# Turning 32x32 tiles of x on VectorE instead of transposing x on TensorE

## What is computed

```python
msg = jnp.concatenate([x[src], edge_attr], axis=1) @ W1 + b1      # (50000, 96) @ (96, 128)
agg = jax.ops.segment_sum(msg, dst, num_segments=100000)
out = jnp.concatenate([x, agg], axis=1) @ W2 + b2                 # (100000, 192) @ (192, 64)
x = _layernorm(x + out, axis=-1)
```

## Time and profile before

| | us |
|---|---|
| median of three runs | 1029.17 |
| lowest, highest | 1028.0, 1034.58 |
| the profiled execution | 1031.75 |
| its span in the profile | 1030.0 |

### The profile page before, as it was taken

How to read it: one execution, slowest core, us unless ns; L and a number is a source line. 1 busy time by engine, 2 the same in 40 slices (tenths; PEclk the granted TensorE clock), 3 DMA queues, 4 the chain that set the end, 5 groups by cost and what they waited for, 6 DMA issues and landing times.

```text
span 1030.0 us, 25989 instructions
## 1 busy us (share of the span) xinstructions
PE 667.1 (65%) x8086; PEld 601.0 (58%) x8087; DVE 411.6 (40%) x945; ACT 446.2 (43%) x2113; POOL 398.7 (39%) x422
## 2 busy tenths in 40 slices
PE   3194557657656775676575677657656756579764
PEld 3174556547646664565475567546646646579753
DVE  7273334334325333333343234533433433337443
ACT  1013434535536454354364346534534534366422
POOL 8664443443443335334434433443443443620000
PEclk8576876876768677677687668867877876678666
DMA  2121322322333223223223223332232332233101
GB/s 62 27 53 40 84 61 66 87 71 66 77 80 98 59 74 88 59 69 91 63 76 87 61 66 85 95 74 68 73 82 61 88 76 57 65 80 90 45 22 42
DMA packets 171918, 71.39 MB, mean 69 GB/s; under 512 B 64737, under 2 KB 165615, under 8 KB 171888
## 3 DMA queue, kind: packets, MB, share of 16 engines
q1 hardware_dynamic: 107728, 51.75, 17.3%
q0 software_dynamic: 12544, 12.87, 6.9%
q10 hardware_dynamic: 51616, 6.41, 4.0%
HBM read 45.37 MB, written 25.60 MB: 69 GB/s over the span
## 4 chain that ended last, share of the span: by engine, by line
PE 61%; issue 31%; DVE 2%; another core or an unknown queue 2%; POOL 2%; DVEq 1%; DMA 0%; ACT 0%; ACTq 0%; POOLq 0%
PE ps_y L549 27%; PE ps_y L540 13%; PE ps_z L468 8%; PE ps_x L529 6%; PE ps_t L460 4%; PE ps_y L586 1%; POOL feat L435 1%; PE ps_x L607 1%; PE ps_y L567 1%; DVE onehot_x L962 1%; DMA feat<-in_x,src_idx 0%; DVEq L962 0%; PE ps_y L607 0%; DVEq L240 0%
## 5 line engine op out<-in xcount | busy, mean ns | idle before, releaser
L435 POOL DMA_INDIRECT feat<-in_x,src_idx x392 | 390.1, 995 | 529.3 <-PE ps_t L460 406.3
L549 PE MATMUL ps_y<-z_window,onehot 128*128 128x64 bf16 x5292 | 292.4, 211 | 285.9 <-issue 282.1
L549 PEld LDWEIGHTS ps_y<-z_window,onehot 128*128 128x128 bf16 x5292 | 240.8, 110 | 337.8 <-issue 328.0
L669 ACT ACTIVATE square<-ps_y 128x64 bf16<-128x64 f32 x784 | 162.6, 240 | 401.8 <-PE ps_y L540 399.8
L932 DVE TENSOR_TENSOR onehot<-node_of_col,dst_in_group 128x2304 bf16<-128x2304 bf16 x98 | 133.2, 1359 | 331.1 <-PE ps_y L540 307.2
L540 PE MATMUL ps_y<-wx,x_t 128*128 128x128 f32 x784 | 155.9, 360 | 6.5 <-issue 6.4
L669 ACT ACTIVATION_READ_ACCUMULATOR square<-ps_y 128x1 f32 x784 | 159.6, 225 | 0.0
L540 PEld LDWEIGHTS ps_y<-wx,x_t 128*128 128x128 f32 x784 | 134.8, 259 | 8.2 <-issue 7.6
L468 PE MATMUL ps_z<-wz,feat_t 97*128 97x64 f32 x784 | 100.6, 285 | 4.5 <-issue 4.5
L468 PEld LDWEIGHTS ps_z<-wz,feat_t 97*128 97x128 f32 x784 | 98.7, 204 | 5.6 <-issue 5.2
L812 DVE TENSOR_TENSOR z<-z_rest,z 128x512 f32 (+1 forms) x49 | 33.9, 691 | 134.1 <-ACT z L657 71.8
(11 more groups left out here) (148 smaller groups left out, 244.2 us busy)
## 6 DMA issues: line engine op xcount, KB each, us to landing
xin<-in_x SPq DMA_DIRECT2D x97, 192.0 KB
out<-yout SPq DMA_DIRECT2D x97, 192.0 KB
xin<-in_x SPq DMA_DIRECT2D x99, 64.0 KB
out<-yout SPq DMA_DIRECT2D x99, 64.0 KB
feat<-in_x,src_idx POOLq DMA_INDIRECT x392
feat<-in_edge_attr ACTq DMA_DIRECT2D x97, 64.0 KB
z<-in_src SPq DMA_DIRECT2D x1, 192.0 KB
z<-in_dst SPq DMA_DIRECT2D x1, 192.0 KB
```

Of the source, the lines that this page charges most:

```text
L435: nc.gpsimd.indirect_dma_start(out=feat[h][:, feat_at(k) + c, 0:C], out_offset=None, in_=x[:, :], in_offset=bass.IndirectOffsetOnAxis(ap=s ...
L549: nc.tensor.matmul(ps_y[h][:, col:col + C], onehot[h][:, slot, a, :], z_window[h][:, slot, part * C:(part + 1) * C], start=False, stop=Fal ...
L669: sq = nc.scalar.activation(square[:, q, :], ps_y[h][:, q * C:(q + 1) * C], ACT.Square, accum_out=sumsq[:, h, q:q + 1])
```

## The change

x is loaded so that its 32x32 tiles only have to be turned around in their places. A row of a tile of x (two nodes, 128 values) is cut into four quarters of 32 values; quarter i of 32 rows goes to partitions 32i to 32i+31, at columns 32m to 32m+31 for rows 32m to 32m+31. VectorE's transpose of 32x32 tiles then gives the 128x128 transpose in one instruction for the whole block (128x512). TensorE's transposes of x, the banks' copies on ScalarE and the semaphore `x_used` are gone; the bank `ps_x` is used in the setup only. A block's load is eight DMAs instead of two (four quarters, low part and high part), each piece 128 bytes long in DRAM instead of 512; the first block has 12 more for its cut part, in place of one. `turn_x` stands in VectorE's unit ahead of each block's one-hots, and waits for the load and for `y_done[h]` of the unit before, since it writes `x_t[h]`. The loads wait for `x_ready[h]`.

```diff
+        def low_squares(b, i):
+            at = (BLOCKS - 1 - b) * GN
+            rows = x[at:at + GN, :].rearrange("(p a) c -> p (a c)", a=A)
+            return rows[:, i * SQ:(i + 1) * SQ].rearrange("(m r) c -> r m c", r=SQ)
+
+        def high_squares(b, i):
+            at = LOW + (BLOCKS - 1 - b) * HIGH * GN
+            groups = HIGH if b > 0 else 1
+            rows = x[at:at + groups * GN, :].rearrange("(p a) c -> p (a c)", a=A)
+            return rows[:, i * SQ:(i + 1) * SQ].rearrange("(m r) c -> r m c", r=SQ)
...
             def load_x(k, h):
                 b = 2 * k + h
-                wait_rounds(sp, x_used[h], k)
-                sp.dma_start(xin[h][:, 0, :], low_part(x, b)).then_inc(x_loaded[h], 16)
+                wait_rounds(sp, x_ready[h], k)
+                for i in range(A * C // SQ):
+                    quarter = xin[h][i * SQ:(i + 1) * SQ, :, :]
+                    sp.dma_start(quarter[:, 0, :].rearrange("r (m c) -> r m c", c=SQ), low_squares(b, i)).then_inc(x_loaded[h], 16)
+                    groups = quarter[:, 1:(G if b > 0 else 2), :].rearrange("r g (m c) -> r (g m) c", c=SQ)
+                    sp.dma_start(groups, high_squares(b, i)).then_inc(x_loaded[h], 16)
...
-            def turn_x(k, h):
-
-                pe.wait_ge(x_loaded[h], 16 * transfers(k + 1, h))
-                wait_rounds(pe, x_ready[h], k)
-                for g in range(G):
-                    tr = nc.tensor.transpose(ps_x[h][:, g * P:(g + 1) * P], xin[h][:, g, :], ident[:, :])
-                tr.then_inc(x_used[h], 1)
...
                 dense(G - 1).then_inc(y_done[h], 1)
-                turn_x(k + 1, h)
...
-            def keep_x(u, h):
-                act.wait_ge(x_used[h], u + 1)
-                nc.scalar.activation(x_t[h][:, :], ps_x[h][:, :], ACT.Copy).then_inc(x_ready[h], 1)
...
                 keep_y(u, 0)
-                keep_x(u + 1, 0)
                 keep_y(u, 1)
                 root(u)
-                keep_x(u + 1, 1)
...
+            def turn_x(k, h):
+
+                dve.wait_ge(x_loaded[h], 16 * x_transfers(k + 1, h))
+
+                dve.wait_ge(y_done[h], k + 1)
+                nc.vector.transpose(x_t[h][:, :], xin[h][:, :, :].rearrange("p g c -> p (g c)")).then_inc(x_ready[h], 1)
...
             def unit(u):
-                one_hots(u, 0)
-                one_hots(u, 1)
+                for h in range(2):
+                    turn_x(u, h)
+                    one_hots(u, h)
                 normalize(u)
```

More of the change, by code:

```diff
@@ L58 @@
 EPS = 1e-5
+SQ = 32
 assert BATCHES == BLOCKS == 2 * PAIRS and 0 <= TWICE < P and BLOCKS <= P and G == 4
@@ L210, in gnn_residual_layernorm @@
         x_loaded = sem2("x_loaded")
-        x_used = sem2("x_transposed")
-        x_ready = sem2("x_t_ready")
+        x_ready = sem2("x_turned")
         hots_used = sem2("onehots_used")
@@ L267, in high_part, with cut_squares, x_transfers @@
             return t[at:at + groups * GN, :].rearrange("(g p a) c -> p g (a c)", g=groups, p=P, a=A)
+        def low_squares(b, i):
[7 more added lines that the diff above has]
+            return rows[:, i * SQ:(i + 1) * SQ].rearrange("(m r) c -> r m c", r=SQ)
+        def cut_squares(i, m, parts):
+            rows = x[CUT:N, :].rearrange("(p a) c -> p (a c)", a=A)
+            return rows[m * SQ:m * SQ + parts, i * SQ:(i + 1) * SQ]
         def cut_part(t):
             return t[CUT:N, :].rearrange("(p a) c -> p (a c)", a=A)
+        def x_transfers(k, h):
+            return 2 * A * C // SQ * k + (A * C // SQ * -(-CUT_PARTS // SQ) if h == 0 and k > 0 else 0) \
+                if isinstance(k, int) else 2 * A * C // SQ * k + A * C // SQ * -(-CUT_PARTS // SQ) * (1 - h)
         def transfers(k, h):
@@ L318, in load_x @@
                 b = 2 * k + h
-                wait_rounds(sp, x_used[h], k)
-                sp.dma_start(xin[h][:, 0, :], low_part(x, b)).then_inc(x_loaded[h], 16)
-                if b == 0:
[L322 to L325, removed]
+                wait_rounds(sp, x_ready[h], k)
[4 more added lines that the diff above has]
+                    sp.dma_start(groups, high_squares(b, i)).then_inc(x_loaded[h], 16)
+                if b == 0:
+                    for i in range(A * C // SQ):
+                        for m in range(-(-CUT_PARTS // SQ)):
+                            parts = min(SQ, CUT_PARTS - m * SQ)
+                            sp.dma_start(xin[h][i * SQ:i * SQ + parts, 2, m * SQ:(m + 1) * SQ],
+                                         cut_squares(i, m, parts)).then_inc(x_loaded[h], 16)
             for h in range(2):
@@ L360, in _ @@
                         load_x(k, h)
-                    else:
-                        sp.wait_ge(x_used[h], PAIRS)
-                        sp.sem_inc(x_loaded[h], 32)
                 if k >= 2:
@@ L611, in _ @@
             pe.wait_ge(s_wready, 3)
-            for h in range(2):
-                turn_x(0, h)
             for h in range(2):
@@ L719, in _ @@
             edge_round(LAG + 1)
-            for h in range(2):
-                keep_x(0, h)
             act.wait_ge(s_opened, 2)
```

## The result

The changed kernel takes 995.88 us (median of four runs, 993.5 to 996.11), beside 1030.87 us (1028.0 to 1034.58) for the kernel before: a ratio of 0.965, 95% interval 0.962 to 0.968. 993 us was forecast.

What follows compares the result with a forecast made beforehand. Each 20.2 us round was taken as GpSimd's gathers with their trail, then TensorE's own work. TensorE 39, last units +2, collisions -2, SyncE -2, start -1 gave 36 us off 1031.75: 996, or 993 as run median; range 975 to 1012.

Steps and rivals of the forecast that it cites:

- TensorE's gain, 0.87 us a unit, 39 us: TensorE's chain without transposes of x: 0.43 us (slow clock) plus 0.44 us a unit, over about 45 units.
- The rival of the full 1.29 us: TensorE's clock rises with work done, not time: 1.29 us gained a unit, 974 us in all; chance 0.17.
- some 6 us after the crawl ended: When TensorE's clock rises, counted from when small matmuls beside the gathers stop coming singly; expected unchanged without the transposes.
- The sign set for the idle time behind a series: Expected in a round's chain: next first gather 0.9 us sooner after the last one's end, 9.1 us for 10.0.
- The last four units, 2 us gained: At the end, four units wait at places for VectorE: 2 us more gained for them, between 0 and 5.
- ScalarE, nothing: ScalarE's 98 removed copies of 0.58 us are not on the chain, so no gain was counted.
- VectorE's transpose, 0.65 us, under cover: VectorE's transpose ahead of the one-hots takes 0.65 us; TensorE needs the windows later, so nothing waits directly.
- The collisions, 0.30 us lost and 0.25 gained a round: Gathers beside later window copies lose 0.30 us, beside later `normalize` gain 0.25: net 0.05 a round, 2 us lost.
- the rival: The gathers eat the gain: copies hit each round's second gather, `normalize` gains nothing, 29 us lost, 1022 us; chance 0.15.
- 2 were allowed for the rounds with two units: SyncE's 8.6 us a unit against some 6.5 without gathers: 2 us lost in two-unit rounds, between 0 and 13.
- The rival of SyncE as the bound: Issues up to 1.37 us make SyncE's unit 24 us against 20.2: 1200 us; chance 0.13 together with another slower rival.
- covered by over 10 us: SyncE's loads for a block, 3.3 us plus a landing, are wanted only a round later, so hidden.

Runs made afterwards that it cites:

- the dead transposes: The changed kernel with four unread TensorE transposes per block put back behind dense: 1.006 of the kernel before at 1044.4 us, 1.122 where that takes 645 us.
- two_loads_2: The changed kernel with x loaded by the old two DMAs a block, node sums wrong: 999.4 us, 0.957 of the kernel before at 1044.4 us.
- two_loads: The changed kernel with x loaded by the old two DMAs a block, node sums wrong: 650.3 us, 1.007 of the kernel before at 645.0 us.

## Why the prediction was right, and where it was not

**What bounds the kernel.** Right for the first condition: a round is the gathers' part plus TensorE's own. I read the crawl as a property of the kernel. It comes with a condition outside it: the same program ran without it. The one row that could have warned is the earlier trace rows itself, where a matmul without a dependence waits 0.29 and 0.49 us on "issue".

**TensorE's gain, 0.87 us a unit, 39 us.** Right: 0.90 us a round between dense and `turn` in the two traces, 0.92 us a unit (41.5 us) by the dead transposes. The argument behind it holds as well: the transposes took 1.30 us of a round, and other matmuls, moved down into the slow stretch, gave 0.43 of it back (forecast: 1.29 and 0.42). The rival of the full 1.29 us is out. What I had from one round only is the place of the rise, "some 6 us after the crawl ended": over the rounds the mean is 5.0 us before and 4.5 after, and it comes no later with less work in front of it. The sign set for the idle time behind a series, 0.9 us less, came out at 1.4 (9.27 and 7.87).

**The last four units, 2 us gained.** Wrong in sign: 5.7 us lost from the 49th series on. I costed them for TensorE and left SyncE out, though its loads stand ahead of `free_yout` there as anywhere; two_loads_2 gives most of it back.

**ScalarE, nothing.** Nothing of it shows: with the copies out and the transposes back, the kernel is not faster than before. No run takes the copies out alone; as the loads cost 9 us of a net 5.7, a few us for ScalarE aren't excluded.

**VectorE's transpose, 0.65 us, under cover.** 0.71 us; TensorE waits for windows 7.3 us in all in the changed kernel, 3.7 before. Covered. In the second condition it and the rest of the change, without the loads, cost 0.7% (two_loads).

**The collisions, 0.30 us lost and 0.25 gained a round.** In the traces: gathers that overlap window copies went from 12 with 5.5 us of stretch to 45 with 21.3, 0.35 us a round lost; those that overlap `normalize` from 75 with 13.3 us to 74 with 8.3, 0.11 gained. Net 0.24 us where 0.05 was written. My reason for 0.30, copies at the gather's start more than at its end, has it the right way round: the later in a gather the copies start, the longer it gets (last section). One of the two long gathers that I set beside the page's rule, the one of 1.40 us, ran beside a product and not a copy.

Whether a longer gather lengthens the round one for one, as the sum and the rival had it, stays open. Over all rounds the series grew by 0.31 us and dense started 0.27 us sooner, which speaks against it; in the rounds in which dense starts behind the last gather the series grew by 0.24 us and dense starts 0.13 us later (0.26 by the medians), which doesn't. The pace of the crawl moves both, and no run holds it still. What is out is the rival's price: with 29 us lost the kernel would have come out at 1022 us. The Trainium skill's page SBUF — State Buffer, section Who interferes with whom, is borne out in that the gather is held up by the copies (1.21 us beside the copies at 591.16). It is not borne out in the order: the page gives the shared ports to whoever issues first, for its whole instruction, and here the gather had begun first and was still the one to wait. In the second condition, where from the 7th series on GpSimd waits for nothing, a longer gather goes into the round in full.

**SyncE.** Issues 0.47 and 0.43 us (medians of L346 and L348), a block 3.9 us instead of 3.3, since I took the low part's issue from the first of a pair. Packets 267,312 for 265,000; the queue's share rose by 8.2 points, as forecast. Cost: 9 us where 2 were allowed for the rounds with two units and 1 for the start.

**The sum.** 39 + 2 - 2 - 2 - 1 = 36; measured 41.5 - 5.7. TensorE's term was right for its reason. The rest was luck in part: the net of the others, 3 us forecast and 5.7 measured, came near although the end was wrong in sign and the loads and collisions were too small.

**The rival of SyncE as the bound** was given a point of decision: 1.1 us an issue against a round of 20.2 us. It came true in the second condition with issues 0.49 us apart, since the round fell to 10.9. That is the step of the prediction that doesn't carry: "covered by over 10 us" took the round of 20.2 us as given. The number that I should have set beside it is how short a round the other engines can make: eight gathers, 10 us, were in the rows.

## What to carry to other kernels

A cost is hidden only as long as the thing that hides it stays slow. Work out each hidden queue (here SyncE: 16 issues and 4 stores, 9.8 us a unit) against the fastest round that the other engines can make, not against the round seen. A stretch of "issue" on the bounding engine is no property of the kernel until runs at other times show it too; before a change is kept that pays on one queue for time on that engine, both kernels want timing where that stretch is gone. And an experiment that takes away a wait can hand the chain to the next queue: compare the time, not the wait.

## What the runs showed of the hardware

- One program, 1030 and 645 us. In the slower condition small matmuls come singly, 0.72 or 1.43 us apart, from some 3 us behind the start of the first gather of a series until 1.3 us behind the end of the last (means of the kernel before); in the other 54 of them take 1.75 us beside gathers. What sets the condition isn't known; it held for whole groups of runs, and the chip with the number 15 showed both.
- A gather of 0.94 us takes longer by a fixed pattern when the four window copies of a block start during it, at least 0.05 us behind its start: in all 848 such cases of the fourteen traces it ended 0.08 us (0.077 to 0.089) ahead of the last copy. So it took 0.95 us with copies that start at once and up to 2.13 us with copies that start at its end; 1.60 us in the earlier trace rows (copies 0.70 us behind its start), 1.70 us at 403.03 (0.80 us behind).
- A gather that starts while one of the products of `normalize` (128x512 float32, two inputs) has been under way for over 0.05 us, and goes on for 0.13 us more, ends 0.82 us behind that product: all 317 cases without window copies in the fourteen traces lie within 0.01 us of it, up to 1.44 us for the gather. A product that begins behind the gather's start costs it nothing. Between 0 and 0.05 us ahead both occur; in two_loads_2, where most begin 0.03 to 0.04 us ahead, the gathers take 0.94 or 0.95 us.
- VectorE's transpose of 32x32 tiles of 128x512 float32 takes 0.69 to 0.71 us.
- An issue on SyncE's queue for a quarter of a block (low part 16 KB, high part 48 KB, in pieces of 128 bytes) takes 0.43 to 0.47 us (0.34 for the first of a row), and no less than one for the whole part. In the row of sixteen they follow one another every 0.49 us.
